# Expert loop: copy of the turned tokens ahead of the second high part, their split between the two gating steps, and the last query block in halves

## What is computed

```python
xn = _layernorm(x, axis=-1)
x = x + _L0_attn_ref(xn, ...) + _L0_ffn_ref(xn, ...)

# attention, of which only the first 512 rows (4 windows) of each sequence are kept
scores = jnp.einsum('bhnqd,bhnkd->bhnqk', qw, kw) / jnp.sqrt(jnp.float32(D))
probs = jax.nn.softmax(scores, axis=-1)
ow = jnp.einsum('bhnqk,bhnkd->bhnqd', probs, vw)
o = o @ w_out + b_out
return o[:, :l, :]

# experts
topk_scores, topk_idx = jax.lax.top_k(scores, TOP_K)
topk_probs = jax.nn.softmax(topk_scores, axis=-1)
h12 = jnp.einsum('btd,ehd->bteh', x, w12)
hidden = jax.nn.silu(h1) * h2
expert_out = jnp.einsum('bteh,edh->bted', hidden, w3)
y = jnp.sum(total_probs[..., None] * expert_out, axis=-2)
```

## Time and profile before

| | |
|---|---|
| median of 3 runs | 746.48 us (746.29 to 747.36) |
| the profiled execution, its own time | 744.41 us |
| its span | 742.7 us |
| busy: PE, PEld | 664.1 us (89%), 515.0 us (69%) |
| busy: DVE, ACT, POOL | 572.3 (77%), 505.2 (68%), 297.9 us (40%) |
| expert loop | about 160 to 537 us of the span |
| mean granted TensorE clock | 0.981 of full speed |

### The profile page before, as it was taken

One profiled execution on the slowest core, in us unless ns is written; L12 is line 12 of the kernel. 1 busy time (PEld: TensorE's weight loads), 2 busy tenths in 40 slices (PEclk: granted clock), 3 DMA queues, 4 the chain that ended last, 5 costly groups with the idle time before them and its releaser, 6 DMA issues.

```text
span 742.7 us, 17175 instructions
## 1 busy us (share of the span) xinstructions
PE 664.1 (89%) x5648; PEld 515.0 (69%) x5649; DVE 572.3 (77%) x907; ACT 505.2 (68%) x880; POOL 297.9 (40%) x329
## 2 busy tenths in 40 slices
PE   0877776969999999999999999999989898999984
PEld 0655564848888878787878787788767676766663
DVE  4869899867777877777777777777857879797883
ACT  4545496566766666676767676767657787888884
POOL 3000470114445444444444454445311335666653
PEclk9999898999999999999999999999999999999998
DMA  8894677641111111111111111111147696875830
GB/s 290 277 261 139 168 269 251 195 173 41 46 54 45 50 47 57 42 49 49 57 42 50 49 54 45 49 49 49 42 135 206 183 263 187 278 197 174 223 118 29
DMA packets 66303, 92.56 MB, mean 125 GB/s; under 512 B 6384, under 2 KB 53360, under 8 KB 66256
## 3 DMA queue, kind: packets, MB, share of 16 engines
q1 hardware_dynamic: 57824, 70.40, 31.8%
q0 software_dynamic: 6864, 18.75, 8.0%
q10 hardware_dynamic: 1568, 2.76, 1.1%
HBM read 59.06 MB, written 32.83 MB: 124 GB/s over the span
## 4 chain that ended last, share of the span: by engine, by line
PE 64%; DVE 14%; ACT 9%; issue 7%; DMA 3%; POOL 2%; ACTq 0%; POOLq 0%; DVEq 0%; SPq 0%
PE PS L1206 57%; PE PS L1450 4%; DVE SMALL L903 4%; ACT WORK L753 3%; DVE XN L1062 2%; PE PS L1428 2%; DVE WALL L897 2%; ACT QS L748 1%; DMA XN<-in_x 1%; DVE WORK L972 1%; DVE WORK L965 1%; DMA KS<-parts_scratch 1%; DVE WALL L921 1%; ACT WORK L691 1%; ACT SIDE L760 1%
## 5 line engine op out<-in xcount | busy, mean ns | idle before, releaser
L350 DVE TENSOR_TENSOR WS<-WALL,WS 128x1024 fp32r<-128x1024 f32 x144 | 176.4, 1226 | 89.2 <-ACT WS L829 88.1
L1206 PE MATMUL PS<-WS,XTS 128*128 128x512 f32 x852 | 234.2, 410 | 2.7 <-DVE XTS L897 1.5
L1206 PEld LDWEIGHTS PS<-WS,XTS 128*128 128x128 f32 x852 | 149.6, 189 | 47.1 <-DVE XTS L897 14.2
L829 ACT ACTIVATE WS<-WALL 128x1024 fp32r x144 | 152.2, 1058 | 39.2 <-issue 36.7
L1206 PE MATMUL PS<-WALL,WORK 128*128 x568 | 136.0, 382 | 0.8 <-ACT WORK L845 0.8
L1206 PEld LDWEIGHTS PS<-WALL,WORK 128*128 128x128 f32 x568 | 102.3, 190 | 12.6 <-issue 1.0
L633 POOL DMA_INDIRECT WORK<-xn_scratch,WORK x72 | 100.8, 1400 | 24.7 <-issue 21.6
L574 POOL TENSOR_TENSOR OTS<-SIDE,XN 128x256 f32<-128x256 f32 x32 | 24.2, 755 | 210.8 <-DVE XN L1062 138.8
L637 POOL DMA_INDIRECT ys_scratch<-SIDE,WORK x36 | 41.9, 1165 | 117.1 <-ACT SIDE L855 117.1
L903 DVE TENSOR_REDUCE SMALL<-PS 128x8 f32<-128x1024 f32 x64 | 77.5, 1210 | 13.2 <-PE PS L1206 13.0
L753 ACT ACTIVATE WORK<-PS 128x512 f32<-128x512 f32 x128 | 69.4, 595 | 22.0 <-PE PS L1206 18.9
(11 more groups left out here) (137 smaller groups left out, 999.4 us busy)
## 6 DMA issues: line engine op xcount, KB each, us to landing
WALL<-in_wexp SPq DMA_DIRECT2D x28, 384.0 KB, 7.3
WALL<-ys_scratch SPq DMA_DIRECT2D x16, 512.0 KB, 7.1
parts_scratch<-WORK SPq DMA_DIRECT2D x32, 240.0 KB, 2.4
QS<-parts_scratch SPq DMA_DIRECT2D x16, 480.0 KB, 4.7
XN<-in_x SPq DMA_DIRECT2D x4, 1024.0 KB, 12.1
xn_scratch<-XN SPq DMA_DIRECT2D x4, 1024.0 KB, 7.5
WALL<-in_x SPq DMA_DIRECT2D x8, 512.0 KB, 5.9
KS<-parts_scratch SPq DMA_DIRECT2D x16, 240.0 KB, 3.9
```

What stands on the lines that cost most here:

```text
L350: eng.tensor_tensor(out=WS[:, 1 - k, half, 1], in0=weights, in1=WS[:, 1 - k, half, 0].bitcast(F32), op=ALU.subtract).then_inc(low_ready[ha ...
L829: act.activation(WS[:, 1 - k, half, 0], weights, ACT.Copy).then_inc(high_ready[half], 1)
L1206: return pe.matmul(o, a, b, start=start, stop=stop)
```

## The change

Three pieces. In the expert loop ACT does `take_xt(j+2)` ahead of the second high part. On DVE `hidden` is cut in two: `gated` (tanh plus one, times h1) and `hidden` (times h2), and `low_xt(j+2)` stands between them. For the last window of the last sequence the reciprocal, the multiplication on POOL and the projection are done in two halves of 128 columns, and the reciprocals stand ahead of `project` of the window before; the four windows of the last sequence are stored with a transfer each.

```diff
--- before.py
+++ after.py
@@ -498,8 +498,11 @@
                         send_later(b - 1 - FIRST_LATER, LATER[b - 1])
             send(LAST - 1)
             send_later(LAST - 1 - FIRST_LATER, LATER[LAST - 1])
-            send(LAST)
-            sp.wait_ge(out_done, 16 * B)
+            for n in range(NWIN):
+                sp.wait_ge(r_free, LAST * NWIN + n + 2)
+                t = LAST * TB + n
+                sp.dma_start(ov[:, t, :], XN[:, t, :]).then_inc(out_done, 16)
+            sp.wait_ge(out_done, 16 * (B - 1 + NWIN))
 
 
         @block.gpsimd
@@ -661,7 +664,14 @@
                         later(b, n)
                     if b >= OWN:
                         own(b, n)
-                    divide(b * NWIN + n)
+                    if b * NWIN + n < B * NWIN - 1:
+                        divide(b * NWIN + n)
+            pool.wait_ge(sides_ready, 2 * B * NWIN)
+            pool.wait_ge(r_full, B * NWIN - 1)
+            for k in range(NC_D):
+                pool.wait_ge(recip_ready, B * NWIN + k)
+                pool.tensor_tensor(out=OTS[:, k, :], in0=SIDE[:, k * P:(k + 1) * P], in1=DENS[:, k * P:(k + 1) * P],
+                                   op=ALU.mult).then_inc(turned_ready, 1)
 
 
         @block.scalar
@@ -864,8 +874,8 @@
                     high_part(j + 2, k, 0, j + 1)
                     take_tanh(j + 1, 1 - k)
                     take_ht(j)
+                    take_xt(j + 2, k)
                     high_part(j + 2, k, 1, j + 1)
-                    take_xt(j + 2, k)
                     take_y(j, k, i)
 
                 tile(0, 0, 0)
@@ -1060,6 +1070,14 @@
                 n = c["O"].add()
                 dve.wait_ge(sides_ready, 2 * n)
                 dve.reciprocal(out=DENS, in_=DENS).then_inc(recip_ready, 1)
+
+            def invert_last():
+
+                n = c["O"].add()
+                dve.wait_ge(sides_ready, 2 * n)
+                for k in range(NC_D):
+                    of = DENS[:, k * P:(k + 1) * P]
+                    dve.reciprocal(out=of, in_=of).then_inc(recip_ready, 1)
 
             def project(b, n):
                 t = b * TB + n
@@ -1148,12 +1166,15 @@
                         dve.wait_ge(xn_out, 64)
                     if u == 1 and pending:
                         project(b - 1, NWIN - 1)
+                    if last and u == UNITS - 1:
+                        invert_last()
                     if u % 2 == 1 and u > 1:
                         project(b, u // 2 - 1)
                 if not last:
                     c["W"].add(NWIN)
                 if ends(b):
-                    invert()
+                    if not last:
+                        invert()
                     project(b, NWIN - 1)
 
             for stage in range(2):
@@ -1167,10 +1188,12 @@
                 low_part(dve, 0, 0, 0)
                 dve.wait_ge(r_free, c["R"].now() + 1)
 
-                def hidden(j, k):
+                def gated(j, k):
                     dve.wait_ge(tanh_ready, j + 1)
                     dve.scalar_tensor_tensor(out=HID[:, k, :], in0=HID[:, k, :], scalar=1.0, in1=bank(2 * k),
                                              op0=ALU.add, op1=ALU.mult).then_inc(g_done, 1)
+
+                def hidden(j, k):
                     dve.wait_ge(g_done, j + 3)
                     dve.wait_ge(h2_full, j + 1)
                     tt(HID[:, k, :], HID[:, k, :], bank(2 * k + 1), ALU.mult).then_inc(hid_done, 1)
@@ -1184,14 +1207,16 @@
                 low_xt(1, 1)
                 low_part(dve, 0, 0, 1)
                 low_part(dve, 1, 1, 0)
+                gated(0, 0)
                 hidden(0, 0)
                 low_part(dve, 1, 1, 1)
                 with dve.Fori(0, SLOT_TILES // 2) as i:
                     for k in range(2):
                         j = 2 * i + k
                         low_part(dve, j + 2, k, 0)
+                        gated(j + 1, 1 - k)
+                        low_xt(j + 2, k)
                         hidden(j + 1, 1 - k)
-                        low_xt(j + 2, k)
                         low_part(dve, j + 2, k, 1)
                 dve.wait_ge(low_ready[1], XS_TILES)
                 dve.sem_inc(phase_done, 1)
@@ -1340,6 +1365,8 @@
                 pe.wait_ge(turned_ready, c["R"].now() + 1)
                 pe.wait_ge(r_free, c["R"].now() + 1)
                 for ch in range(NC_D):
+                    if c["R"].now() == B * NWIN - 1 and ch:
+                        pe.wait_ge(turned_ready, B * NWIN + ch)
                     last = mm(R_BANK[:, 0:D], OTS[:, ch, :], WOUT[:, ch, :], ch == 0, ch == NC_D - 1)
                 last.then_inc(r_full, 1)
                 c["R"].add()
```

## The result

| | median, us | runs (lowest to highest) |
|---|---|---|
| before | 746.88 | 4 (746.29 to 747.36) |
| changed | 735.12 | 4 (735.05 to 735.47) |

The ratio is 0.9844, with a 95% interval of 0.9827 to 0.9861: 11.8 us less by the medians, 10.4 to 12.9 us by the interval. The profiled executions took 744.41 and 735.47 us, with spans of 742.7 and 733.7 us: 9.0 us less.

The account below looks back on a forecast made before the run. PE was taken to bound the kernel, with waits for XTS in the expert loop; 6.9 us from the loop plus 2.2 us from the end, 9.1 us, gave 737.4 us, range 734.5 to 743.5 us.

Parts of the forecast that it names:

- The wait for XTS: Expert loop: PE's 34 waits for the tokens' low part, 12.27 us in all, would go, gaining 6.9 us.
- 0.20 us a pass: Expert loop: what PE wins per two-tile pass when its 0.36 us wait goes.
- the gap of 0.16 us that I left to PE: Expert loop: part of each 0.36 us wait that stays as PE's own gap, 5.4 us over 34.
- A pace under 5.20 us: Expert loop: sign of a wrong prediction, PE taking less than 5.20 us from tile to tile.
- The added wait: Expert loop: second high and low parts now wait behind the token copy; cost 0, margins 0.09 and 0.18 us.
- Rivals 2 and 3: Loop: second low part becomes the wait, 739.4 to 744.3 us, chance 0.20; or chain slower than before, 752.8 us, chance 0.07.
- Rival 1: Expert loop: PE gains all 0.27 us a pass, total 735.1 us; chance 0.12.
- the argument against it: Expert loop: 0.07 us a pass belongs to `take_ht`, ahead of the load of `down`, and stays.
- The end: Last window and stores: projection 1.12 us earlier and last store 1.1 us shorter, together 2.2 us.
- The store: End of kernel: last store of 128 KB instead of 512 KB, 1.1 us less, bounds 0.5 to 1.5 us.
- The releaser: End of kernel: last projection's start bound by DVE's addition of window 2, not by POOL.
- the forecast's own band: Whole kernel: 736.2 to 739.4 us, where the forecast itself, without its rivals, had chance 0.56.

Follow-up runs that it names:

- e4: Kernel before with only DVE's reordering in the expert loop (`low_xt` between the two gating steps): 737.44 us, 0.9884 of before.
- e3: Kernel before with only ACT's move in the expert loop (`take_xt` ahead of the second high part): 745.09 us, 0.9990 of before.
- e10: Changed kernel with both ACT loads of the expert's number moved ahead of waits and the loop rotated, its branch under the first high part: 732.76 us, 0.9831 of before.
- e6: Changed kernel with one extra, unused load of the expert's number on ACT behind the copy of the tokens: 760.70 us, 1.0214 of before.
- e11: Changed kernel with DVE's addition of window 2 put ahead of the two half reciprocals at the end: 734.98 us, 0.9863 of before.
- e0: Kernel before, run once more with no edit: 743.72 us in its one run.
- e9: Changed kernel, run once more with no further edit: 734.50 us, 0.9863 of before.
- e1: Kernel before with only the ACT and DVE moves of the expert loop, the end as before: 737.78 us, 0.9884 of before.
- e7: Kernel before with only the last sequence's result stored by four transfers of 128 KB: 744.25 us, 0.9984 of before.
- e8: Changed kernel with ACT's expert loop over four tiles a pass instead of two, removing every second branch: 735.31 us, 0.9870 of before.
- e5: Changed kernel with ACT's load of the expert's number for the second high part ahead of the token copy: 734.44 us, 0.9871 of before.

## Why the prediction was right, and where its terms were off

**The wait for XTS goes: right.** All 34 of them, and e4 and e3 show that it goes by DVE's move alone. The prediction had both moves work together: it timed `low_xt` behind the earlier copy and never priced DVE's move alone. `low_xt` doesn't need it: with the copy left where it was, `low_xt` still ends 0.26 us before its load in the one tile, and no load of the loop waits for it in the other. That step was wrong, and cost nothing.

**0.20 us a pass: a little small.** Measured 10.67 - 10.445 = 0.225 us; over the stage 7.6 us, where 6.9 was reckoned. The term that was mis-sized is the gap of 0.16 us that I left to PE; it measured 0.36 - 0.225 = 0.14 us. The tile that waited fell from 5.41 to 5.18 us, not to its neighbour's level of before; the other one kept 5.26. A pace under 5.20 us, which the prediction named as a sign of being wrong, is there by a hair: e10 has 5.18 to 5.19 us in every tile, so PE's own pace was taken 0.02 us too long.

**The added wait costs nothing: right,** with margins of 0.12 and 0.18 us for 0.09 and 0.18. e6 shows that it was a near thing: 0.53 us more on this chain turn a gain of 10 us into a loss of 16. But this wait bought nothing, as DVE's move alone gives the gain (e4). Rivals 2 and 3 hung on the size of one step, the 0.66 us from copy to high part, for which the prediction had 0.68 from rows without a branch.

**Rival 1, PE gains all 0.27 us: not what happened,** though the median of 735.12 us is the one it gave; that agreement is chance. `take_ht` behind the branch kept its 0.07 us, as the argument against it said, and e10, in which they go, bears it out.

**The end, 2.2 us: 2.5 us in the traces.** The projection starts 2.22 us after the last copy's end, where it was 734.20 to 737.64, 3.44 us: 1.2 us earlier for 1.12 predicted. The store gave 1.2 us for 1.1. (The chain in the prediction is added up from 734.22 and not from the 734.3 it names; from there it would be 1.04.) The releaser is the addition, as predicted; moving it ahead (e11) costs 0.4 us and, with the clock that falls there, 0.7. What the sum lacked is the clock: up to 0.95 us more (2.07 to 2.08 against 1.13) in executions in which it falls before the last matmuls are over.

**The total.** 9.1 us predicted; the edits measure 10.1 us in the traces, 11.0 with the fallen clock. The two intervals are 10.4 to 12.9 and 9.0 to 11.5 us; both hold 11.0, and the second holds 10.1 too. So 735.12 us is within the range, and below the forecast's own band of 736.2 to 739.4. The two profiled executions differ by 9.0 us in span, almost the 9.1 predicted, but that is luck: 10.1 us gained, less 1.1 us in stages that the edits hardly touch. Something of the first comparison stays open: the front of one and the same kernel differs by 1.3 and 2.2 us between traces (159.8 before, 158.5 in e0; 160.6 changed, 158.4 in e9), and no run here tells why.

## What to carry to other kernels

When the bounding engine waits for the last step of a row, try the order within that row first, and each move by itself: here one engine's reordering was the whole gain, and the other's only shifted margin. A load of a register between two instructions of ACT stands behind the first one's wait, so put it ahead of whatever waits where the chain is short of time; on the row behind the loop's branch this, with the branch under the high part, was worth 2.5 us more. At the end of a kernel a shorter chain can give more than its length, if PE's last work is then done before the clock falls.

## What was not expected of the hardware

**The clock at the end.** After 3.10 us of idle PE the last four matmuls took 1.13, 1.51, 1.70, 2.07, 2.07 and 2.08 us in six traces; after 1.89 us they took 1.10 us in all seven. Counted from the end of the matmuls ahead of that idle stretch, the clock fell after 1.95, 2.64, 2.94, 3.52, 3.72 and 4.40 us in the six (e1, e3, e7, e0, e4, before), and after 3.67 to 5.11 us in the seven. The last four end 4.2 us behind that point in the six and 3.0 us in the seven. So part of the gain is only that they are over sooner; that the shorter idle stretch also puts the fall off is what the seven later falls suggest, and no run changed that stretch alone.

**The branch of a longer loop.** ACT's idle time behind the branch grew from 0.66 to 0.76 us when the body was twice as long (e8). Whether it is the length or what the body holds was not tried.

**GpSimd's indirect transfers take longer while DVE's `low_part` runs.** The scatters from OTS, first in the kernel before, then in the changed one:

```profile
L637 POOL DMA_INDIRECT ys_scratch<-OTS,WORK x35: 987/987/1004, 175.8 to 538.4; - x35
...
L640 POOL DMA_INDIRECT ys_scratch<-OTS,WORK x35: 1557/1564/1571, 176.6 to 531.6; - x35
```

The median went from 0.99 to 1.56 us, and POOL's busy time from 297.9 to 346.6 us. One of each, behind the `low_part` that was running when it began (that of the changed kernel is the one at 405.81 above):

```profile
398.55 1.23 DVE L350 TENSOR_TENSOR WS<-WALL,WS 128x1024 fp32r<-128x1024 f32 x1
...
399.74 0.99 POOL L637 DMA_INDIRECT ys_scratch<-OTS,WORK  x1 [1.97 <-ACT OTS L855]
...
406.34 1.56 POOL L640 DMA_INDIRECT ys_scratch<-OTS,WORK  x1 [1.77 <-ACT OTS L865]
```

In the first, `low_part` has 0.04 us left, in the second 407.04 - 406.34 = 0.70 us: 0.97 us plus what is left, less 0.12 us, gives 1.55 us for the second (measured 1.56), and the first stays at its least. The rule held to 0.03 us for all 123 scatters and gathers between 200 and 520 us of the changed kernel, and for the 60 in the kernel before with over 0.13 us left; the 30 that began with no `low_part` under way took 0.97 us, though one started 0.3 us behind them. The rule has an exception in e4 and e5: 39 that began less than 0.05 us after a `low_part` took 0.97 us too. What differs between `low_part` and DVE's other instructions here is that both its inputs are in SBUF. That the others, which read one from PSUM, hold nothing up rests on few cases: a gather that began at 160.2 with 0.32 us of `low_xt` left took 0.95 us. The GPSIMD Engine Reference of the Trainium skill (Specifications) names contention with DVE instructions that have two SBUF inputs, and the traces agree, with up to 0.9 us for one issue. Nobody waits for these transfers here. Each changed order of the loop moves them against `low_part`, which is why they took 1.29 us in e4 and 1.18 us in e10.
